# Mixing two batches in front of the sampling, offsets one batch in front

## What is computed

```python
# block 0, "mixing": xf = normalised x, 128 x 1024
xn = xf / max(norm over channels, 1e-8)
s  = relu(einsum('bcp,bcq->bpq', xn, xn)) ** 2
y  = einsum('bpq,bcq->bcp', s, W @ xf + b)
x1 = x + y
# block 1: xd = normalised x1
offset = conv3x3(conv3x3(xd, w1, b1), w2, b2)      # 72 channels: 4 groups, 9 taps, dy and dx
out    = x1 + relu(deform_conv(xd, offset, wd))    # bilinear samples of 9 taps, then a 128 x 1152 product
```

## Time and profile before

| | us |
|---|---|
| runs | 525.17, 526.4, 526.4; median 526.4 |
| profiled execution | 523.97, its span 522.2 |
| TensorE busy (matmul) | 431.7 (83%) |
| VectorE busy | 347.7 (67%) |
| ScalarE busy | 225.4 (43%) |
| GpSimd busy | 133.3 (26%) |
| mean granted TensorE clock | 0.938 |

### The profile page before, as it was taken

One profiled execution on the slowest core, in us unless ns is written; L12 is line 12 of the kernel. 1 busy time (PEld: TensorE's weight loads), 2 busy tenths in 40 slices (PEclk: granted clock), 3 DMA queues, 4 the chain that ended last, 5 costly groups with the idle time before them and its releaser, 6 DMA issues.

```text
span 522.2 us, 10672 instructions
## 1 busy us (share of the span) xinstructions
PE 431.7 (83%) x3881; PEld 311.6 (60%) x3881; DVE 347.7 (67%) x582; ACT 225.4 (43%) x404; POOL 133.3 (26%) x179
## 2 busy tenths in 40 slices
PE   2898477589969779799979779899988797888876
PEld 2664344456647567676647558586656466656655
DVE  4638883699779854956569954956559947599300
ACT  2134222045554532345545542336555534178640
POOL 3275300038600020027620020016631010031100
PEclk9999688689998987999998988899999899999999
DMA  4400000100000020111000021101010012022111
GB/s 129 157 1 1 0 0 11 35 21 21 21 22 21 22 59 12 28 48 26 21 21 21 21 38 30 31 31 28 16 40 21 21 31 67 22 51 63 41 33 33
DMA packets 22188, 17.27 MB, mean 33 GB/s; under 512 B 1980, under 2 KB 20668, under 8 KB 22140
## 3 DMA queue, kind: packets, MB, share of 16 engines
q1 hardware_dynamic: 21884, 16.07, 11.7%
q10 hardware_dynamic: 256, 0.52, 0.7%
HBM read 3.74 MB, written 3.28 MB: 13 GB/s over the span
## 4 chain that ended last, share of the span: by engine, by line
PE 65%; DVE 17%; ACT 7%; issue 5%; DMA 3%; SPq 1%; DVEq 0%; ACTq 0%; POOL 0%
PE psB L488 14%; PE psB L680 12%; PE psA L558 10%; PE psA L488 7%; PE psT L634 6%; PE psV L656 5%; PE psB L521 3%; PE psA L526 3%; DVE wpix L1262 3%; PE psT L624 2%; DMA hwin<-hwin 2%; ACT wcell L840 2%; DVE combo L1060 2%; PE psA L535 2%; ACT hwin L833 1%
## 5 line engine op out<-in xcount | busy, mean ns | idle before, releaser
L840 ACT ACTIVATE wcell<-psT 128x512 f32<-128x512 f32 (+1 forms) x160 | 84.2, 551 | 113.6 <-PE psT L634 109.2
L1262 DVE TENSOR_TENSOR wpix<-tent 128x512 f32<-128x512 f32 (+1 forms) x160 | 108.4, 731 | 31.0 <-PE psT L634 28.4
L634 PE MATMUL psT<-ident,wpix 128*128 128x128 f32 x576 | 87.5, 282 | 18.3 <-ACT wcell L840 8.7
L403 POOL TENSOR_TENSOR sim<-rel 128x512 f32<-128x512 f32 x64 | 78.6, 1248 | 93.3 <-ACT rel L803 93.3
L634 PEld LDWEIGHTS psT<-ident,wpix 128*128 128x128 f32 x576 | 67.3, 144 | 45.2 <-issue 26.7
L428 POOL COPY strips<-hring 128x256 f32<-128x256 f32 x64 | 36.5, 599 | 140.0 <-PE psT L624 139.8
L680 PE MATMUL psB<-val,wd_sb 128*128 128x256 f32 x288 | 67.3, 391 | 3.6 <-ACT val L853 1.8
L680 PEld LDWEIGHTS psB<-val,wd_sb 128*128 128x128 f32 x288 | 55.0, 195 | 14.4 <-issue 6.8
L558 PE MATMUL psA<-sim,scratch 128*128 128x512 f32 x128 | 60.8, 599 | 0.9 <-ACT inv_all L794 0.7
L488 PE MATMUL psB<-g_p 128*128 128x512 f32 x192 | 58.5, 443 | 0.0
L656 PE MATMUL psV<-wcell,hwin 64*32 64x144 f32 x2048 | 47.4, 294 | 5.2 <-DMA hwin<-hwin 5.2
(11 more groups left out here) (143 smaller groups left out, 445.6 us busy)
## 6 DMA issues: line engine op xcount, KB each, us to landing
hwin<-hwin SPq DMA_DIRECT2D x64, 128.0 KB, 2.4
out<-yout SPq DMA_DIRECT2D x16, 128.0 KB, 1.8
x_all<-x SPq DMA_DIRECT2D x1, 1536.0 KB, 9.6
off_scr<-sim SPq DMA_DIRECT2D x4, 288.0 KB
combo<-sim SPq DMA_DIRECT2D x20, 32.0 KB
val<-w SPq DMA_DIRECT2D x1, 576.0 KB
wd_sb<-wd SPq DMA_DIRECT2D x1, 576.0 KB
x_all<-x SPq DMA_DIRECT2D x1, 512.0 KB, 3.5
```

The source lines that it names most:

```text
L403: pool.tensor_tensor(sim[:, i % 2, j * HALF:(j + 1) * HALF], rel[:, j, :], rel[:, j, :], ALU.mult)\
L634: last = pe.transpose(bank[:, at:at + P], wpix[:, t % 2, k, 2 * h:2 * h + 2, :].rearrange("p g q -> p (g q)"), ident[:, :])
L840: act.activation(wcell[:, t % 2, taps[0]:taps[-1] + 1, :, :].rearrange("q k h p -> q (k h p)"), bank[:, 0:len(taps) * G // 2 * P], ACT.Cop ...
L1262: dve.tensor_tensor(w, ty, tx, ALU.mult).then_inc(s["weights_done"], 1)
```

## The change

- `front` is parted in `mix_front` (slots 0 to 26) and `conv_front` (statistics' mean to offsets). Pass b now has the sampling of b, `mix_front` of b+2, `conv_front` of b+1 and the preparation of b+3.
- In the passes `conv_front` stands earlier (table STEADY): mean 23, spread 24, variance 25, norm 28, combinations 29 and 42, convolutions 35 and 48, wrap 54, shift 56, turns 60 and 61. The weights of tiles 5 to 7 and the preparation move to match. In VectorE's order the norm (28) comes behind `add_mixed` of b+2 (26).
- The prologue does batch 0 as before, and in addition the mixing of batch 1 (table SECOND gives the slot of each of its steps), with its preparation at slots 18 to 33 (PREP_SECOND). Batch 2 is prepared at 57 to 66 (PREP_THIRD).
- Batch 1's mixing uses lent buffers: `wcell` for image, squares, gx and diagonal, `wpix[:, 1]` for `sim`, psT for scores and psV for sums. Hence new waits at the start of pass 0: TensorE's first turns wait for the last ReLU of batch 1, ScalarE's first copy and TensorE's first samples for its addition.
- New waits keep the buffers apart in the passes: mean after the next mixing's last ReLU, convolutions after its `scaled_done`.
- All loops over passes are unrolled. Normalisation of x1 has its own columns `gmean`, `grstd`. SyncE issues the offset shifts one crossing earlier.

```diff
@@ tables
-        STATS, MEAN, VAR, NORM = 26, 31, 33, 34
-        COMBINE, CONV = (35, 46), (40, 51)
-        WRAP_OFF = 57
-        PREP = {57: "normalise", 58: "square", 59: "norms", 60: "invert", 61: "bias", 67: "diagonal"}
-        SPREAD, KEEP = 1, 2
+        SPREAD, KEEP, STATS = 1, 2, 26
+        LEAD = dict(mean=31, dev=31, var=33, norm=34, combine=(35, 46), high=(35, 46), conv=(40, 51), wrap=57,
+                    shift=57, turn={59: (0, 1), 61: (2, 3)}, extremes=65)
+        STEADY = dict(mean=23, dev=24, var=25, norm=28, combine=(29, 42), high=(30, 43), conv=(35, 48), wrap=54,
+                      shift=56, turn={60: (0, 1), 61: (2, 3)}, extremes=66)
+        PREP_FIRST = ("normalise", "square", "high", "norms", "low", "invert", "bias", "diagonal")
+        PREP_SECOND = {18: ("normalise",), 21: ("square",), 22: ("high",), 23: ("norms", "low"), 24: ("invert",),
+                       27: ("diagonal",), 33: ("bias",)}
+        PREP_THIRD = {57: ("normalise", "square"), 58: ("norms", "invert"), 59: ("bias",), 64: ("high",), 65: ("low",),
+                      66: ("diagonal",)}
+        PREP = {55: ("normalise", "square"), 57: ("high", "low"), 58: ("norms", "invert"), 59: ("bias",),
+                67: ("diagonal",)}
+        SECOND = {26: (0,), 32: (3,), 34: (1, 2, 4), 38: (6,), 46: (7,), 49: (9,), 57: (10, 12, 13), 58: (15, 16),
+                  60: (18, 19), 62: (21, 22), 63: (25,), 64: (26,)}
         W_AT = {2: (0, 1, 3, 5, 6), 3: (9, 10, 12, 14, 15), 4: (18, 19, 21, 23, 24),
-                5: (39, 39, 40, 41, 42), 6: (43, 43, 52, 53, 53), 7: (54, 54, 55, 55, 55)}
-        TURN_OFF = {63: (0, 1), 64: (2, 3)}
-        FIRST_WEIGHTS, EXTREMES = 64, 66
-        REST = (SCORE[5], SCORE[7])
+                5: (31, 32, 33, 35, 36), 6: (37, 38, 40, 44, 45), 7: (47, 48, 50, 51, 52)}
+        LEAD_WEIGHTS, FIRST_WEIGHTS = 60, 62
+        REST = (SCORE[4], SCORE[5])
@@ lent buffers
+        lent = wcell[:, :, :, :, :].rearrange("p e k h q -> p (e k h q)")
+        lent_sim = wpix[:, 1, :, :, :].rearrange("p k g q -> p (k g q)")[:, 0:2 * NPIX].rearrange("p (e n) -> p e n", e=2)
+        own_tiles = Mixing(inv2_all[:, :], gsq, gxT, inv2_diag, sim, psB, psA, scratch[:, :])
+        lent_tiles = Mixing(lent[:, 0:NPIX], lent[:, NPIX:2 * NPIX],
+                            lent[:, 2 * NPIX:3 * NPIX].rearrange("p (i c) -> p i c", c=C),
+                            lent[:, 3 * NPIX:4 * NPIX].rearrange("p (i q) -> p i q", q=P), lent_sim, psT, psV,
+                            lent[:, NPIX:2 * NPIX])
+        def tiles(b):
+            return lent_tiles if b == 1 else own_tiles
@@ TensorE, group_mean
+                if b > 0 and col == 0:
+                    pe.wait_ge(s["orelu_done"], 4 * (b - 1) - 1 + ORELU0)
+                    if b + 1 < B:
+                        pe.wait_ge(s["rel_done"], 2 * QT * (b + 2) - 1)
@@ TensorE, conv_front
+                if n == at["conv"][0]:
+                    if b == 0:
+                        pe.wait_ge(s["w_lo_done"], V * len(w_parts))
+                        pe.wait_ge(s["inv2_all_done"], 2)
+                    else:
+                        pe.wait_ge(s["pos_done"], 4 * b)
+                        pe.wait_ge(s["orelu_done"], 4 * (b - 1) + ORELU0)
+                        if b + 1 < B:
+                            pe.wait_ge(s["scaled_done"], 2 * (b + 2))
+                            pe.wait_ge(s["rel_done"], 2 * QT * (b + 2))
@@ TensorE, turns
+                if b == 0 and t == 0 and idx < 2:
+                    pe.wait_ge(s["rel_done"], 2 * QT * 2)
@@ TensorE, sample
+                if b == 0 and n == 0:
+                    pe.wait_ge(s["scaled_done"], 4)
@@ ScalarE, evacuate
+                if b == 0 and t == 0 and idx == 0:
+                    act.wait_ge(s["scaled_done"], 4)
@@ TensorE, order of a pass
+                        if b + 2 < B:
+                            mix_front(b + 2, n)
+                        if prep is not None:
+                            for what in PREP.get(n, ()):
+                                prepare(prep, what)
                         if nxt is not None:
-                            front(nxt, n, prep)
+                            conv_front(nxt, n, STEADY, prep)
@@ TensorE, prologue and passes
             for n in range(SLOTS):
-                front(0, n, 1)
+                mix_front(0, n)
+                for b, table in ((1, PREP_SECOND), (2, PREP_THIRD)):
+                    for what in table.get(n, ()):
+                        prepare(b, what)
+                conv_front(0, n, LEAD, 2)
+                for step in SECOND.get(n, ()):
+                    mix_front(1, step)
-            with pe.Fori(0, B - 2) as b:
-                batch_steps(b, b + 1, b + 2)
-            batch_steps(B - 2, B - 1, None)
-            batch_steps(B - 1, None, None)
+            for b in range(B):
+                batch_steps(b)
@@ VectorE, order of a pass
-                            front(nxt, n, prep)
+                            conv_front(nxt, n, STEADY)
@@ SyncE
+            for b in range(B):
+                for t in range(ROWT - 2):
                     cross(b, t)
-                shift_offsets(b + 1)
+                if b + 1 < B:
+                    shift_offsets(b + 1)
+                cross(b, ROWT - 2)
                 store(b, 0)
                 cross(b, ROWT - 1)
```

More of the change, by code:

```diff
@@ L457, in batch_steps @@
                         n = K * t + k
[L458 to L459 removed]
+                        if b + 2 < B and n in SCORE:
+                            square(b + 2, SCORE.index(n))
+                        if nxt is not None and n == STEADY["wrap"]:
+                            wrap_offsets(nxt)
                         if t < ROWT - 1 and k == 5:
@@ L516, in prepare @@
             def prepare(b, what):
+                own = tiles(b)
                 if what == "norms":
@@ L906, in _ @@
             first_std(0, 1)
-            for what in PREP.values():
+            for what in PREP_FIRST:
                 prepare(0, what)
             for n in range(SLOTS):
-                front(0, n, 1)
+                mix_front(0, n)
+                for b, table in ((1, PREP_SECOND), (2, PREP_THIRD)):
+                    for what in table.get(n, ()):
+                        prepare(b, what)
+                conv_front(0, n, LEAD)
+                for step in SECOND.get(n, ()):
+                    mix_front(1, step)
                 if n == REST[1]:
```

270 lines of the change are left out of this document (153 added, 117 removed).

## The result

The changed kernel takes 520.66 us in the median (four runs, 519.88 to 521.13) where the kernel before takes 526.4 (four runs, 525.17 to 529.74): a ratio of 0.988, with a 95% interval of 0.9833 to 0.9926. It is faster by 1.2%, a quarter of what was forecast: 5.7 us and not some 24, and the time lies outside the range of 493 to 513. The profiled execution took 520.94 us, span 519.2, against 523.97 and 522.2 before.

The account below looks back on a forecast made before the run. TensorE was taken as the bound, busy 431.71 of 522.2 us, with 90.5 idle to fill. Prologue +19.0, pass 0 -4.0, pass 1 -10.3 and pass 2 -27.6 sum to -22.9: forecast 502 us, range 493 to 513.

Parts of the forecast that it names:

- the DMA chain of the offsets: End of pass 1, last output to first turn: named as what is late next, 1.3 us of wait.
- (a): Prologue: batch 1's norms ahead of batch 0's last mixing product cost 7.1 us, 0.4 covered: +6.7.
- Step (e): Prologue's end: TensorE's remaining batch 1 work, batch 2's norms, then VectorE's work put batch 2's spread at 126.5: +16.3.
- Step (c): Prologue: spread, mixing product and score of batch 1 fill the 4.40 us gap; convolution 1 starts 9.3 us later, at 70.0.
- (d): Prologue: product and score fill the 3.59 us gap before convolution 2; convolutions' matmuls speed up by 1.7 and 1.4.
- rival (2): Prologue: VectorE and GpSimd exclude each other; contention's upper bound 9, not 2.7, plus score waits: 510 to 512, chance 0.08.
- Pass 0's early half: Pass 0 through the convolutions: convolution 1 ends 3.1 us earlier, convolution 2 3.5, its outputs 3.7.
- the term of 34 us by VectorE's order: Pass 2 after slot 26: spread, normalisation, combinations, sums and three tiles take 34 us; last outputs end at +49.7.
- (1): Rival: VectorE's order eats the early chain; passes 0 and 1 gain only the norms: 511 to 513, chance 0.14.
- (3): Rival: clock stays at its upper level throughout the prologue and contention misses: 490 to 495, chance 0.08.
- (4): Rival: in the prologue TensorE waits for each step of batch 1, +53: about 535, chance 0.05.
- (5): Rival: pass 0's first turns wait on lent buffers until the fill is given back: 525 to 528, chance 0.03.

Follow-up runs that it names:

- e1: Changed kernel with SyncE's last crossing of windows issued ahead of the first store of outputs: 503.85 us.
- e2: Changed kernel with the next batch's first weights at slot 64 again, behind VectorE's first output: 503.78 us.
- e12: e5 with four of the nine offset shift transfers issued by ScalarE again: 503.97 us.
- e5: Changed kernel with last crossing ahead of the store, all nine shift transfers on SyncE, first weights at slot 64, turns at 62 and 63: 491.33 us.
- e4: Kernel before with its pass loops written out as straight code and nothing else: 520.2 us.
- e11: e5 with the first tile's weights of the next pass at slot 62 again: 495.05 us.
- e6: e5 with the low part of batch 2 made ahead of VectorE's addition of mixing 1 in the prologue: 498.05 us.
- e10_unrolled_again: Kernel before with its pass loops written out, timed a second time with more rounds: 521.03 us.

## Why the prediction was wrong, step by step

**The step that failed most** is the one in the passes where I wrote that what is late next "is the DMA chain of the offsets" and followed VectorE's and TensorE's slots only to the last outputs and the first turn. I took the tail over from the kernel before, in pass 2 as the 29.2 us of the earlier trace rows plus small terms, and in passes 0 and 1 without a term of its own. But the change reorders this tail: the first weights at slot 62 were in the diff, and I costed their move on VectorE alone. I did not walk SyncE's queue behind it, where the store waits for VectorE's output and the crossing behind the store. e1 and e2 put it at 17 us of the missing 18.7 (502 forecast, 520.66 measured): the passes gave +0.5, -2.5 and -13.5 where I had -4.0, -10.3 and -27.6. That e1 then stands at 503.85, near the forecast, is luck and no proof of the rest: the points below are errors of both signs that happen to cancel.

**The transfers of the shift** were a second miss of the same kind. I gave the offsets' DMA chain 1.3 us of wait in pass 1 and 0.5 in pass 2. In after TensorE waits 3.49 and 3.48 us for the copy behind ScalarE's issues, with the slow stretch behind (e12: some 10 to 12.6 us if nothing else covers it). I counted the transfers' flight and not their issue time on the engine that issues them. This is what keeps e1, at 503.85, from the 491 of e5: e12, which is e5 with these issues, is at 503.97. The other new wait, for the copy behind which the strips are turned (first row of the waits: 17.9 us in 26, before 11.8 in 14), was not in the forecast either, and no run takes it away: it is 16.5 in e1 and 15.4 in e5.

**The prologue** was priced too dear by 7 us. (a) The norms of batch 1 were priced at 7.1 us from the earlier trace rows, at a low clock. In after they run between mixing products at the upper level, and take 1.95 + 2.03 with overlapping ends:

```profile
48.16 1.95 PE L553 MATMUL psT<-ones,wcell 128*128 128x1 f32 x16
49.97 2.03 PE L559 MATMUL psV<-w_sb,wcell 128*128 128x128 f32 x16
```

The statistics' product came at 57.97, not 61. Step (e) used the same price for the norms of batch 2, which took 1.84 and 2.03 (94.94, 96.64). Two times some 3.4 us is nearly all of the 7. Step (c) put the convolution at 70.0; it began at 67.61. (d) Its 18 matmuls took 4.55 us and those of the second 4.65, where I had expected 6.37 - 1.7 = 4.7 and 6.03 - 1.4 = 4.6: right. TensorE was busy 43.46 of the 46.50 us between 57.7 and 104.2, at a mean clock of 0.96, against 30.23 at 0.76. (e) The end of the prologue waits for VectorE, as I wrote, though the profile shows the wait one step earlier, 7.07 us at score 0. VectorE's addition, reductions and diagonal took what I had. The contention with GpSimd's squares is where it was expected, in tile 0's five weight products, 4.52 us (2.8 undisturbed, 435.56 in after: 2.83). That is 1.7, and the second and third step of the tents ahead of them, beside squares as well, took 1.48 + 1.18 where they take 0.76 + 0.46 (426.46, 427.26). Together 3.1, near the 2.7 taken and far from the 9 of the exclusive rule; rival (2) falls.

**The norms in the passes.** In pass 1 of the kernel before they did run at the low clock, behind a wait:

```profile
310.92 3.58 PE L521 MATMUL psB<-ones,rel 128*128 128x1 f32 x16 [3.09 <-ACT rel L787]
314.36 3.45 PE L526 MATMUL psA<-w_sb,inv_all 128*128 128x128 f32 x16
```

So taking them out of pass 1 was priced about right at 7.1. What the forecast left out is pass 0, where they stay: in after they take 1.95 + 2.03 there, behind 0.69 (200.42), which is some 3 us less work and 2.4 less wait. The forecast had the smaller wait, called little of it new gain, and left the price of the norms as it was.

**Pass 0's early half** was right. From the last product of mixing to the end of the second convolution it takes 38.4 us in after and 41.65 before, 3.2 less where I had 3.5. That, and what the norms gave back, was then lost in the tail, which holds the wait of 4.31.

**Pass 2** was right as a mechanism: with the queues out of the way and the turns later (e5) it takes 86.5 us from first turn to first turn, which is within my mark of 88, and is 23.7 shorter, between the bounds of -22 and -30 around -27.6. The missing 4 us lie ahead of the last outputs, which end at +54.5 and not +49.7: the term of 34 us by VectorE's order took 38.5 (353.08 to 391.55), and VectorE stood still in it for ScalarE's high part (1.79 at 358.45) and for TensorE's convolution (2.88 at 388.14). In after pass 2 was 96.7, and that was the sign I had named for a wrong prediction.

**Unrolling** at 0, bounds -1 and +1: wrong. I compared pass 2 and pass 1, 9.0 us apart, and explained all of it by the norms and their wait, 9.4 us. But pass 2 ends behind a step that the others don't have, a matmul on `farthest` at 456.46 with a wait of 1.25 for VectorE. It made pass 2 1.5 us longer by my marks. From pair to pair the two are 10.4 us apart (119.11, 108.72), and 8.7 in e4 (117.48, 108.80), where both are straight code. The 1.6 us of the loop was hidden by that step.

**The rivals.** (1), VectorE's order eats the gain, came nearest in kind, since it is VectorE's order that starts it. But it had the wrong victim, the next normalisation and not the store and the crossing, and only 511 to 513. Of (3) the clock of the prologue nearly came true (0.92 where it was 0.74), and the contention did not miss. (4) and (5) did not happen: TensorE did not wait for single steps of batch 1, and the first turns of pass 0 did not wait for lent buffers.

## What to carry to other kernels

When a step is moved ahead of another on one engine, list what waits for the step that is now later, and for each waiter what is queued behind it on its own engine, DMA issuers first: an in-order queue that waits for a store holds every load behind it. Price matmuls that will be moved by rows with the upper clock where they will stand between busy work, and a wait of several us by the slow stretch behind it too. And where two waits stand in a row, taking away one shows little (2.7 us) until both are gone (12.6 us). Before a difference between two kernels is put down to an edit, see whether it lies at the instructions that the edit touches: that of e5 and e11 did not.

## What the runs showed of the hardware

The clock that TensorE is granted is a cost of waits, and a large one: 18 matmuls took 6.07 us after a wait of 4.08, and 6.46 after one of 3.50, where they take 4.16 without. After 2.04 us the same stretch of the program went either way, at a mean granted clock of 1.00 in the profiled execution of e5 and 0.82 in that of e6. The full level is 2.4 GHz, and the means between are time spent at 1.2. The start differs by execution too. These are the first spread and score, and the statistics of batch 0 behind its mixing, of the unrolled kernel in e4_unrolled_before and then in e10_unrolled_again, one program run twice:

```profile
22.34 1.98 PE L535 MATMUL psA<-combo,ones 128*128 128x512 f32 x4 [3.18 <-DVE combo L1014]
23.76 1.95 PE L488 MATMUL psB<-g_p 128*128 128x512 f32 x6
...
52.70 0.59 PE L513 MATMUL psB<-mv,avg 128*128 128x1 f32 x2 [4.38 <-DVE mv L960]
```

```profile
22.54 3.78 PE L535 MATMUL psA<-combo,ones 128*128 128x512 f32 x4 [3.04 <-DVE combo L1014]
25.33 3.40 PE L488 MATMUL psB<-g_p 128*128 128x512 f32 x6
...
55.70 0.58 PE L513 MATMUL psB<-mv,avg 128*128 128x1 f32 x2 [4.37 <-DVE mv L960]
```

The start alone makes them 3.0 us apart, after a wait of some 3 us in both. The Trainium skill ("TensorE: Matmul & The Clock Gate", section "What's actually happening") says of slow matmuls at a kernel's start that their number is "run-variable"; these rows agree. The rows of pass 1 above (275.52 in e5, 278.34 in e6, 273.80 in e11) show a like difference in the middle of a kernel. A stage that holds such a wait carries 1 to 3 us of chance, which no slot table shows.
